# Causal attention on one core: the two narrow units of each diagonal joined, the row maxima's transfer asked for one unit earlier, the context store behind it, and VectorE adding the probability tiles of the last group

## The reference, cut to what matters

```python
# 32 query heads, 8 key/value heads of 32 features, T = 1024 tokens, 2 batches
att = einsum('bhgqd,bhkd->bhgqk', q, k) / sqrt(32)
att = where(causal, att, -inf)
probs = softmax(att, axis=-1)
ctx = einsum('bhgqk,bhkd->bhgqd', probs, v)
x = x + ctx @ Wo
```

## Time and profile before

| | |
|---|---|
| median of 3 runs | 1596.94 us (1595.2 to 1599.36) |
| the profiled execution | 1599.63 us, its span 1597.9 us |
| PE busy | 1543.1 us, 97% of the span |
| DVE, ACT, POOL busy | 959.9, 587.2, 657.7 us |
| attention, from its first row to its last products | about 565 to 1171.9 us of the span |

### The profile page before, as it was taken

The page is one execution under the profiler, slowest core; times in us unless marked ns, Lnnn a source line. Parts: engine busy times, 40 slices in busy tenths (PEclk is TensorE's granted clock), DMA queues, the critical chain, the costliest instruction groups (busy, mean ns, idle before and its releaser), DMA issues. The chain is left out here.

```text
span 1597.9 us, 26436 instructions
## 1 busy us (share of the span) xinstructions
PE 1543.1 (97%) x9312; PEld 1197.6 (75%) x9312; DVE 959.9 (60%) x2723; ACT 587.2 (37%) x1185; POOL 657.7 (41%) x403
## 2 busy tenths in 40 slices
PE   7999998899999979999999999999989999999999
PEld 7999998788888845555555555555458999999998
DVE  6545454546463368888888888888437334343433
ACT  4333333211121115566666665666623121212210
POOL 1222122433343306777777777777832101010100
PEclk9999999999999959999999999999989999999999
DMA  6332333342322352334333333440133121212200
GB/s 227 122 110 94 121 113 135 126 133 94 104 104 81 119 108 67 81 98 100 85 75 74 74 81 82 101 101 29 48 143 135 40 80 42 79 53 65 68 25 40
DMA packets 118776, 145.97 MB, mean 91 GB/s; under 512 B 40977, under 2 KB 77073, under 8 KB 118385
## 3 DMA queue, kind: packets, MB, share of 16 engines
q1 hardware_dynamic: 90064, 120.59, 26.1%
q10 hardware_dynamic: 28592, 23.86, 4.6%
HBM read 95.66 MB, written 53.51 MB: 93 GB/s over the span
## 5 line engine op out<-in xcount | busy, mean ns | idle before, releaser
L1485 ACT ACTIVATE at_probs<-ps 128x512 f32<-128x512 f32 (+3 forms) x768 | 324.7, 494 | 154.2 <-PE ps L1401 152.1
L1554 DVE CUSTOM_DVE_ANT_0 ps<-ps,at_score_mask 128x512 f32<-128x512 f32 (+3 forms) x512 | 291.0, 618 | 39.4 <-PE ps L1390 36.4
L1339 POOL TENSOR_TENSOR at_added<-at_added,at_probs 128x2048 f32<-128x2048 f32 (+1 forms) x64 | 224.0, 3500 | 2.3
L329 POOL TENSOR_TENSOR f_x_ring<-f_x_ring,f_half_bias 128x1024 f32<-128x1024 f32 x32 | 77.1, 2412 | 311.3 <-DVE f_h L590 310.8
L1401 PE MATMUL ps<-at_qs,at_ks 98*128 98x512 f32 (+3 forms) x528 | 192.9, 392 | 4.6 <-ACT at_probs L1485 2.9
L1390 PE MATMUL ps<-at_ks,at_qs 96*128 96x512 f32 (+3 forms) x528 | 177.6, 372 | 11.6 <-DMA at_ks<-scr_k_hi 10.9
L1401 PEld LDWEIGHTS ps<-at_qs,at_ks 98*128 98x128 f32 x528 | 97.9, 194 | 111.9 <-ACT at_probs L1485 85.5
L1416 PE MATMUL ps<-at_probs,at_vs 128*32 128x512 f32 (+3 forms) x1536 | 165.5, 503 | 4.0 <-POOL at_probs L1319 4.0
L1554 DVE CUSTOM_DVE_ANT_0 ps<-ps,at_score_mask,at_part_max 128x128 f32<-128x128 f32 (+3 forms) x256 | 133.3, 556 | 14.0 <-issue 9.6
L48 PE MATMUL f_ps<-f_wt_hi,f_hT_hi 128*128 128x400 f32 (+1 forms) x384 | 134.5, 350 | 3.2 <-DVE f_hT_lo L594 3.2
L49 PE MATMUL f_ps<-f_wt_lo,f_hT_hi 128*128 128x400 f32 (+1 forms) x384 | 131.6, 343 | 0.0
(11 more groups left out here) (161 smaller groups left out, 3123.3 us busy)
## 6 DMA issues: line engine op xcount, KB each, us to landing
at_qs<-scr_q_hi SPq DMA_DIRECT2D x20, 512.0 KB, 6.1
f_x_ring<-in_L_attn_resid SPq DMA_DIRECT2D x16, 512.0 KB, 3.6
x<-f_x_ring SPq DMA_DIRECT2D x16, 512.0 KB, 2.7
early<-x SPq DMA_DIRECT2D x16, 512.0 KB, 3.3
scr_q_hi<-qkv_rope_hi ACTq DMA_DIRECT2D x32, 256.0 KB, 2.0
scr_q_lo<-qkv_rope_lo ACTq DMA_DIRECT2D x32, 256.0 KB, 2.3
scr_ctx<-at_ctxn SPq DMA_DIRECT2D x32, 256.0 KB, 2.4
shared<-scr_ctx SPq DMA_DIRECT2D x16, 512.0 KB, 4.5
```

Of the source, the lines that this page charges most:

```text
L329: pool.tensor_tensor(x_ring[:, u, :], x_ring[:, u, :], half_bias[:], ALU.add).then_inc(bias_added, 1)
L1339: pool.tensor_tensor(added[:, heads, :], first, probs[:, u % PROBS, heads, :], ALU.add).then_inc(added_done, 1)
L1485: act.activation(probs[:, u % PROBS, g, 0:z - a], score_ps[(u * G + g) % BANKS][:, 0:z - a], ACT.Exp, scale=SCALE).then_inc(exp_done, 1)
L1554: dve.tensor_tensor_reduce(out=src, in0=src, in1=mask, scale=1.0, scalar=part_max[:, g, own] if c else -3.0e38, op0=ALU.add, op1=ALU.max, ...
```

## The change

- Units 2 and 3 of half 0 become one unit `(0, (2, 3))`, and units 10 and 11 one unit `(1, (6, 7))`: 256 and 128 queries side by side in one bank and one tile, 384 wide. A group has 10 units, 0 to 2 and 3 to 9. PE issues two score matmuls and then two sets of products for a joined unit; ACT takes one exponential over 384, POOL one mask over both triangles (128 x 1024 elements, where one had 128 x 512). The tiles added together are the same key blocks, now units 3 to 7.
- The rows of group m are spread over unit 9 of group m-2 and units 0 to 8 of group m-1. `TURN_B` of group m-1 stands behind the fourth item of that unit 9, ahead of the sums of half 1; so it comes one unit earlier than before.
- `store(n-1, 0)` now follows `load_rows(n, 1)` in SP's queue.
- POOL's additions stand in units 2, 3, 5, 6 and 7, `divide(n, 0)` in 8, `low_wo` in 9. In the last group POOL adds nothing: DVE does (`add_last`), four additions over 128 x 2048 elements.
- The first product by Wo waits for one sum to be read, the second for the other.

```diff
-    ADDED = range(4, 9)
-    ADDS_TO = {4: 1, 5: 1, 6: 2, 7: 3, 8: 5}
+    ADDED = range(3, 8)
+    ADDS_TO = {3: 1, 4: 1, 5: 2, 6: 3, 7: 5}
...
-        units = [(half, j) for half in range(2) for j in range(QH * (half + 1))]
+        units = [(0, (0,)), (0, (1,)), (0, (2, 3))] + [(1, (j,)) for j in range(NQ - 2)] + [(1, (NQ - 2, NQ - 1))]
...
+        for m in range(2, NG + 1):
+            windows = [(m - 2, NU - 1)] + [(m - 1, u) for u in range(NU - 1)]
+            for at, items in zip(windows, spread(first, weight, [room[u] for _, u in windows])):
+                placed[at] = of(m, items) if m < NG else []
+            lead = placed[m - 2, NU - 1]
+            lead.insert(min(SLOTS, len(lead)), (m - 1, TURN_B))
...
                 load_rows(n, 1)
+                if n:
+                    store(n - 1, 0)
...
-                tile = probs[:, u % PROBS, :, 0:P]
+                tile = probs[:, (NU * n + u) % PROBS, :, :].rearrange("p g (b n) -> p g b n", b=2)[:, :, 0:count, 0:P]
...
-                    if u in (3, 4, 6):
-                        add(n, (5, 6, None, 7)[u - 3])
-                    if u in (7, 8):
-                        add(n, 8, slice(G // 2 * (u - 7), G // 2 * (u - 6)))
+                    if n < NG - 1 and u in (2, 3, 5):
+                        add(n, (4, 5, None, 6)[u - 2])
+                    if n < NG - 1 and u in (6, 7):
+                        add(n, 7, slice(G // 2 * (u - 6), G // 2 * (u - 5)))
...
+                for j, at, cols in blocks(u):
+                    last = pe.matmul(score_ps[x % BANKS][:, cols], ks[:, nm, j * P:(j + 1) * P], qs[nm][0:KROWS + 2, half, g, at],
+                                     start=True, stop=True)
...
+            def add_last(u):
...
+                dve.tensor_tensor(added[:], first, probs[:, (NU * (NG - 1) + u) % PROBS, :, :], ALU.add).then_inc(last_added, 1)
...
+                    if n == NG - 1 and u in (3, 4, 5, 6):
+                        add_last(u + 1)
```

More of the change, by code:

```diff
@@ L1145, in attention_stage, with blocks, width @@
         ctx_stored = [sem(f"ctx_stored{h}") for h in range(2)]
-        units = [(half, j) for half in range(2) for j in range(QH * (half + 1))]
+        units = [(0, (0,)), (0, (1,)), (0, (2, 3))] + [(1, (j,)) for j in range(NQ - 2)] + [(1, (NQ - 2, NQ - 1))]
         NU = len(units)
[L1149 to L1158, removed]
+        H0 = QH - 1
+        LAST = {H0 - 1: 0, NU - 1: 1}
+        LAST_OF = (H0 - 1, NU - 1)
+        APART = (range(H0), range(ADDED[-1] + 1, NU))
+        def blocks(u):
+            half, js = units[u]
+            out, at = [], 0
+            for j in js:
+                a = max(j * P - half * HALF, 0)
+                out.append((j, slice(a, HALF), slice(at, at + HALF - a)))
+                at += HALF - a
+            return out
+        def width(u):
+            return blocks(u)[-1][2].stop
+        diagonal = [u for u in range(NU) if units[u][1][0] >= units[u][0] * QH]
         rows = [("row", i, g, c) for i in range(NQ) for c in range(i // QH + 1) for g in range(G)]
@@ L1199, in attention_stage @@
         early = rows[OPEN + 8:OPEN + 20]
[L1200 to L1207, removed]
+        for u in range(H0):
+            placed[0, u] = of(0, early[4 * u:4 * u + 4])
+        for u, items in enumerate(spread([TURN_A] + rows[at_a:], weight[at_a:], room[H0:NU - 1])):
+            placed[0, H0 + u] = of(1, items)
+        for m in range(2, NG + 1):
[3 more added lines that the diff above has]
+            lead = placed[m - 2, NU - 1]
+            assert len(lead) >= SLOTS or m == NG
+            lead.insert(min(SLOTS, len(lead)), (m - 1, TURN_B))
+        placed[NG - 1, NU - 1] = []
         for n in range(NG):
@@ L1215, in attention_stage @@
             for u in range(NU):
-                if n == 0 and u in (0, QH):
-                    for key in BEFORE[u // QH] + [key for part in BETWEEN[u // QH] for key in part]:
+                if n == 0 and u in (0, H0):
+                    for key in BEFORE[u // H0] + [key for part in BETWEEN[u // H0] for key in part]:
                         number[key] = len(number)
@@ L1303, in _ @@
                     store(n - 1, 1)
-                store(n, 0)
+            store(NG - 1, 0)
             store(NG - 1, 1)
@@ L1334, in add @@
                     pool.wait_ge(unit_done, NU * n + NU)
-                    first = probs[:, ADDED[0] % PROBS, heads, :]
+                    first = probs[:, (NU * n + ADDED[0]) % PROBS, heads, :]
                 else:
@@ L1412, in products @@
                     pe.wait_ge(exp_done, NU * G * n + (G * (u + 1) + BANKS))
-                if j == 0:
+                if js[0] == 0:
                     pe.wait_ge(ctx_copied, 2 * n + (half + 1))
-                for g in range(G):
-                    last = pe.matmul(ctx_ps[g * DH:(g + 1) * DH, at], vs[:, n % RING, j, :], probs[:, u % PROBS, g, 0:z - a],
-                                     start=j == 0, stop=u in LAST)
+                for j, at, cols in blocks(u):
+                    for g in range(G):
+                        last = pe.matmul(ctx_ps[g * DH:(g + 1) * DH, at], vs[:, n % RING, j, :],
+                                         probs[:, (NU * n + u) % PROBS, g, cols], start=j == 0, stop=u in LAST and j == js[-1])
                 last.then_inc(unit_done, 1)
@@ L1430, in sums @@
                 for u in APART[half]:
-                    a, z = queries(u)
-                    for g in range(G):
-                        last = pe.matmul(out[g * DH:(g + 1) * DH, a - half * HALF:z - half * HALF], ones[:],
-                                         probs[:, u % PROBS, g, 0:z - a], start=u == 0, stop=u in LAST)
+                    for j, at, cols in blocks(u):
+                        for g in range(G):
+                            last = pe.matmul(out[g * DH:(g + 1) * DH, at], ones[:], probs[:, (NU * n + u) % PROBS, g, cols],
+                                             start=u == 0, stop=u in LAST and j == units[u][1][-1])
                 last.then_inc(slot_filled, 1)
```

98 lines of the change are left out of this document (55 added, 43 removed).

## The result

The changed kernel takes 1582.05 us (median of 4 runs, 1580.26 to 1582.36) against 1596.49 for the kernel before in the same runs; the ratio is 0.9908, with a 95% interval from 0.9890 to 0.9925. The forecast was 1580. The profiled execution took 1582.36 us, its span is 1580.6.

A forecast was written before the change was run, and what follows sets the result against it. PE's own queue was taken to bound the kernel, with POOL close behind. Gains of 4.8 (steady groups), 1.4 (late transfers), 9.9 (last group) and 1.0 (group 0) made 17.1 us, from 1596.94 to 1580; range 1572 to 1589.

The forecast's parts named there:

- Part 4: DVE's rows squeezed from twelve units into ten: waits taken as zero, upper bound 0.9 + 0.55 us (units 4 and 1).
- Part 3: Maxima of half 1 turned a unit ahead, store behind the transfer: 1.4 us of lateness goes, the store's order brings nothing.
- Rival 4: DVE binds and gets slower: PE waits 0.9 in unit 4, 0.55 in unit 1; 1601.6 us or more; chance 0.05.
- Part 1: Joined units on PE: 0.8 us less in each group, so PE alone would have a period of 34.6 us.
- Part 2: Steady groups: PE waits 0.5 us for POOL at every sum of half 1; period 35.1, gain 4.8 us over 14.
- rival 2: Steady groups gain nothing, the wide mask taking 1.55 or DVE costing 0.35 a group: 1585 us; chance 0.15.
- Part 5: Last group, with DVE adding and joined pairs: 9.9 us gained, 8.6 of it from POOL's work and the lower clock.
- Rival 3: Last group: DVE's additions and POOL's masks lock each other, two meetings exposed, 4.6 us: 1584.5 us; chance 0.06.

The follow-up runs named there:

- recip_u3: The changed kernel with DVE's reciprocals of half 0 behind the rows of unit 3 instead of unit 4: 1578.38 us, ratio 0.9896.
- turn_recips: turn_later with DVE's reciprocals of the half 1 before behind the rows of unit 0 instead of unit 1: 1567.21 us, ratio 0.9828.
- turn_later: The changed kernel with recip_u3's edit, POOL's addition of unit 6 one unit earlier and TURN_A four rows later: 1569.06 us, ratio 0.9844.
- spread_alone: The kernel before with only the new dealing of the rows and the turn of half 1 in the last unit: 1602.95 us, ratio 1.0054.
- store_ahead: The changed kernel with store(n-1, 0) ahead of load_rows(n, 1) in SP's queue again: 1582.32 us, ratio 0.9918.
- tail_alone: The kernel before with only DVE's additions in the last group: 1588.22 us, ratio 0.9959.

## Why the prediction was right, and where not

**The time** came out 2 us over the forecast, inside the range. Against the first profile of the kernel before, the span is 17.3 us shorter, nearly the 17.1 of the sum; but that is luck, for 5.6 of it (2.1 ahead of the attention, 3.5 in group 0) is what two executions of the kernel before differ by. Against the second profile it's 13.3: 0.4 ahead of the attention, then 1.4, 1.6 and 10.0 by stretch, and -0.1 behind. The medians differ by 14.4. The steady groups gave 1.0 to 1.6 of the 6.2, so the time hit the forecast more closely than its largest uncertain term did.

**Part 4 is the step that failed**: "four slots lie between, so I take the waits as zero and the excess, 0.9 + 0.55, as the upper bound". Measured: the excess of unit 4 costs 0.58 a group (`recip_u3`), that of unit 1 0.22 (`turn_recips`), 0.80 of 1.45. The slots don't carry the whole excess over: the last row of unit 5 waits for one of them, so it's paid in the step behind the reciprocals. `TURN_A` where it stands costs another 0.24 (`turn_later`). And the new dealing has a cost that neither Part 3 nor Part 4 had: by `spread_alone` it's 0.6 a group with narrow units, where Part 3 counted only the 1.4 us of late transfers as a gain. Rival 4's argument against itself, that the reciprocals have full rows behind them today and PE is busy, looked only behind them: ahead of them, in the same unit, stood four rows of 128 and one of 512, and after the change four of 512 and one of 256.

**Part 1** was right in size, and a little low. With nearly all waits taken out the period is 34.37 where I had 34.6 for PE alone, 1.0 below the kernel before instead of 0.8. That is the join together with the new dealing and four later moves of the order; the join by itself was only measured with DVE's waits on both sides, 0.6.

**Part 2** was right in mechanism, and hidden. POOL is a wall at 35.19 (35.1 forecast), with a wait of 0.3 at the sums (0.5 forecast) and a mask of 1.07 to 1.14 (1.2 taken). But it shows only once DVE's wait is gone. Rival 4 put DVE's waits outside the stretch that POOL covers, where they would have been added to POOL's; the wait of 0.58 is inside it, behind the last score of unit 7, and there the longer of the two hides the other. PE's 11.3 for that stretch was thus 12.0 in the changed kernel. The sign forecast, sums that wait for POOL in every group, was absent but for group 0 (0.53) and group 14 (0.17). What happened in the steady groups was rival 2, by the mechanism of rival 4 at half its price: 35.40 - 34.60 = 0.8 of gain eaten.

**Part 3**: the late transfers went, as said; the store did nothing, as said (`store_ahead`).

**Part 5**: 30.08 us from the sums to L48 where 30 were expected. Additions of 2.25 to 2.32, as taken. The split was off: taking them back costs 8.7 (8.6 forecast), the join is worth 31.65 - 30.08 = 1.6 (0.8 forecast: 0.6 + 0.5 - 0.3), and a new wait of 0.44 ahead of L48 stands against it. The terms don't add up freely, as `tail_alone` with 5.0 shows, since its 35 us hold seven at the lower clock and the wait of 0.92.

**Rival 3** was the right mechanism at a small price. The mask at 1146.35 took 1.36 beside DVE's addition, which ran from 1144.87 to 1147.16; a mask of the same size took 0.68 at 1144.16, with no addition running. PE's rows show no wait for it. The Trainium skill (SBUF — State Buffer, "Who interferes with whom") has a DVE instruction with two inputs in SBUF contend with a GpSimd instruction that reads SBUF, for ports that only one of them holds at a time; the trace agrees, for the mask ends 0.55 after the addition, which is most of its own 0.68. I had priced a meeting at a whole addition, 2.3; in this one the mask grew by 0.68, where 0.81 of the addition remained. Another meeting may be the exposed one: POOL's division at 1149.89 took 2.25 beside DVE's split of the context, 1.28 without, so the piece of Wo behind it ended at 1153.37, 0.10 ahead of L48, for which the kernel has PE wait. The profile names no releaser for the 0.44 there, and no run tests it.

## What to carry to other kernels

When work is taken out of a saturated engine's queue by joining steps, the work of the other engines is squeezed into fewer steps as well: count each helper's load step by step, by the sizes of what stands ahead of its longest piece of work and not only behind it, and take an excess as paid in the next step unless an edit of the order shows otherwise. A wall that a trace doesn't show may stand right behind the one that it does; two edits that each bring little (0.24 and 0.0 a group) brought 0.6 together. And profile the kernel before twice before a difference in one stretch is put down to the change.

## What the runs showed of the hardware that I hadn't expected

- The length of the lower clock at the start of a stage differs between executions of one unchanged kernel: 37.5 and 27.3 us at 0.50, with 3.5 us between the two times to the first sums. Over all profiles here it was 23.9, 27.3 or some 37.
- A turn, a small transpose of 0.28 us on PE, costs 0.24 a group or nothing, by which rows stand around it, probably because it holds one of four slots until another engine has read it; the reason itself wasn't tested.
- A mask over twice the elements took 1.07 from start to start and the narrow one 0.65 (875.23 to the next start at 875.88), so about 0.2 is fixed (an estimate, 2 x 0.65 - 1.07).
